# Mix-matrix strips made of three products each, two of them in column halves of the array

## The reference

```python
attn = einsum('ds,td->st', w1, w2) * sparse_mask        # 1024 x 1024, masked to a band
y    = einsum('bds,st->bdt', x, attn) + b2
x    = layernorm(x + gelu(y))
w_l  = dequant_kbit(qweight, lut4, 4)                   # 1024 x 1024 from 4 bit planes
w_h  = dequant_kbit(qweight, lut8, 8)
y    = where(norm(x) > 64, x @ w_h.T, x @ w_l.T) + bias
x    = layernorm(x + y)
```

## Time and profile before

| what | value |
|---|---|
| median of 3 executions | 307.67 us (307.31 to 307.9) |
| profiled execution, its own time | 306.75 us |
| its span | 304.9 us |
| PE busy | 289.1 us, 95% of the span |
| DVE busy | 196.3 us, 64% |
| ACT busy | 183.8 us, 60% |
| strip products (line 430) | 128 matmul records, from 5.00 to 35.11 us |
| mean granted TensorE clock | 0.994 of full speed |

### The profile page before, as it was taken

How to read it: one execution, slowest core, us unless ns; L and a number is a source line. 1 busy time by engine, 2 the same in 40 slices (tenths; PEclk the granted TensorE clock), 3 DMA queues, 4 the chain that set the end, 5 groups by cost and what they waited for, 6 DMA issues and landing times.

```text
span 304.9 us, 5064 instructions
## 1 busy us (share of the span) xinstructions
PE 289.1 (95%) x1907; PEld 254.0 (83%) x1907; DVE 196.3 (64%) x351; ACT 183.8 (60%) x244; POOL 108.8 (36%) x179
## 2 busy tenths in 40 slices
PE   7899889999999999999999999999999999999990
PEld 3688666676668999999999999999998888888880
DVE  2679998997858979798776785504035345344362
ACT  1965658888988968977895979342144453312210
POOL 4000003343343989898788100000033333323321
PEclk9999999999999999999999999999999999999997
DMA  6999998999999411011101111118237775443222
GB/s 222 398 355 354 379 383 265 244 255 231 206 186 202 93 35 37 34 37 34 37 34 38 52 38 52 53 37 231 115 121 250 264 257 200 170 157 153 103 111 107
DMA packets 28480, 49.78 MB, mean 163 GB/s; under 512 B 2464, under 2 KB 11936, under 8 KB 28448
## 3 DMA queue, kind: packets, MB, share of 16 engines
q1 hardware_dynamic: 23536, 40.79, 38.8%
q0 software_dynamic: 4352, 8.39, 15.3%
q10 hardware_dynamic: 560, 0.20, 0.2%
HBM read 36.79 MB, written 12.58 MB: 162 GB/s over the span
## 4 chain that ended last, share of the span: by engine, by line
PE 78%; DVE 10%; ACT 3%; issue 3%; DMA 3%; SPq 1%; POOL 1%; POOLq 0%; DVEq 0%; ACTq 0%
PE acc L559 19%; PE acc L561 19%; PE acc L560 19%; PE acc L542 5%; PE acc L430 3%; PE acc L488 3%; DMA w<-in_w2d 3%; PE acc L498 2%; PE acc L463 2%; PE acc L464 2%; PE acc L465 2%; DVE zz L1033 2%; DVE dest L991 1%; ACT z L706 1%; PE acc L475 1%
## 5 line engine op out<-in xcount | busy, mean ns | idle before, releaser
L559 PE MATMUL acc<-lin,zz 128*128 128x256 f32 (+2 forms) x424 | 130.4, 307 | 0.3 <-issue 0.3
L561 PE MATMUL acc<-lin,zz 128*128 128x256 f32 (+2 forms) x424 | 130.0, 307 | 0.0
L560 PE MATMUL acc<-lin,zz 128*128 128x256 f32 (+2 forms) x424 | 129.8, 306 | 0.0
L559 PEld LDWEIGHTS acc<-lin,zz 128*128 128x128 f32 x424 | 80.0, 189 | 4.6 <-issue 0.5
L560 PEld LDWEIGHTS acc<-lin,zz 128*128 128x128 f32 x424 | 80.3, 189 | 4.0
L561 PEld LDWEIGHTS acc<-lin,zz 128*128 128x128 f32 x424 | 80.2, 189 | 4.1
L724 ACT ACTIVATE leaf<-planes,lut,flip 128x1024 f32<-128x1024 uint8 x56 | 67.4, 1237 | 0.6 <-DVE dest L991 0.6
L991 DVE COPY_PREDICATED leaf<-planes,leaf 128x1024 f32<-128x1024 uint8 x32 | 43.4, 1355 | 12.0 <-ACT leaf L724 11.2
L1374 POOL DMA_DIRECT2D z<-in_xr x16 | 19.7, 1237 | 72.0 <-ACT z L706 70.1
L826 ACT ACTIVATE junk<-rows,cols 128x1024 bf16<-128x1024 f32 x15 | 17.2, 1150 | 41.3 <-POOL cols L1348 41.3
L1346 POOL TENSOR_TENSOR cols<-cols 128x1 f32<-128x1 f32 x15 | 9.5, 634 | 79.2 <-DVE rows L1109 79.2
(11 more groups left out here) (108 smaller groups left out, 431.9 us busy)
## 6 DMA issues: line engine op xcount, KB each, us to landing
z<-in_xt SPq DMA_DIRECT2D x16, 512.0 KB, 9.1
z<-in_xr POOLq DMA_DIRECT2D x16, 512.0 KB, 8.7
out_rows<-rows SPq DMA_DIRECT2D x15, 512.0 KB, 2.9
out_rows<-parts SPq DMA_DIRECT2D x32, 128.0 KB, 1.7
rows<-out_rows SPq DMA_DIRECT2D x16, 256.0 KB, 2.6
w<-in_w1d SPq DMA_DIRECT2D x7, 512.0 KB, 8.9
off_band<-in_mask_rest SPq DMA_DIRECT2D x8, 448.0 KB, 4.2
w<-in_w2d SPq DMA_DIRECT2D x3, 584.0 KB, 9.6
```

What stands on the lines that cost most here:

```text
L559: nc.tensor.matmul(bank, hi, w_hi, start=k == 0, stop=False)
L560: nc.tensor.matmul(bank, hi, w_lo, start=False, stop=False)
L561: last = nc.tensor.matmul(bank, lo, w_hi, start=False, stop=k == KB - 1)
```

## The change

Each strip's product with 272 columns is replaced by three: `strip_own`, all 128 rows of the strip with its own 128 columns; and in `strip_beside` up to two products whose weights are only 64 columns wide, rows 0 to 63 of the strip with the left 72 columns and rows 64 to 127 with the right 72. Their outputs lie on PSUM partitions 0 to 63 and 64 to 127, so they use the left and the right column half of the array. Strips 0 and 7 have one side product only. All own products of a row block of d stand together, and so do all side products; even row blocks begin with the own ones, odd row blocks with the side ones, so that the array changes between full width and half width once per row block and group of strips.

```diff
--- before.py
+++ after.py
@@ -425,29 +425,40 @@
                                             start=d == 0, stop=d == KB - 1)
                 last.then_inc(e_made, 1)
 
-            def strip_row(b, d):
-                first, end = strip_of(b)
-                return nc.tensor.matmul(unit_bank(b)[:, places_of(b)], w1[:, d, b * P:(b + 1) * P], w2[:, d, first:end],
-                                        start=d == 0, stop=d == KB - 1)
-
-            def front_strips():
-                starts = [first for first, _ in ROW_PIECES]
-                for d in range(KB):
-                    if d in starts:
-                        pe.wait_ge(w_loaded[starts.index(d)], 32)
-                    for b in range(FRONT):
-                        last = strip_row(b, d)
+            def strip_own(b, d):
+                return nc.tensor.matmul(unit_bank(b)[:, REACH:REACH + P], w1[:, d, b * P:(b + 1) * P],
+                                        w2[:, d, b * P:(b + 1) * P], start=d == 0, stop=d == KB - 1)
+
+            def strip_beside(b, d):
+                if b:
+                    nc.tensor.matmul(unit_bank(b)[0:SIDE, 0:REACH], w1[:, d, b * P:b * P + SIDE],
+                                     w2[:, d, b * P - REACH:b * P], start=False, stop=False)
+                if b + 1 < KB:
+                    nc.tensor.matmul(unit_bank(b)[SIDE:P, REACH + P:STRIP], w1[:, d, b * P + SIDE:(b + 1) * P],
+                                     w2[:, d, (b + 1) * P:(b + 1) * P + REACH], start=False, stop=False)
+
+            def strips(rows, bands):
+                for d in rows:
+                    if d % 2:
+                        for b in bands:
+                            strip_beside(b, d)
+                    for b in bands:
+                        last = strip_own(b, d)
                         if d == KB - 1:
                             last.then_inc(mix_made, 1)
+                    if d % 2 == 0:
+                        for b in bands:
+                            strip_beside(b, d)
+
+            def front_strips():
+                for n, piece in enumerate(ROW_PIECES):
+                    pe.wait_ge(w_loaded[n], 32)
+                    strips(range(*piece), range(FRONT))
 
             def back_strips(n):
-                for d in range(KB):
-                    if d % HALF_BLOCKS == 0:
-                        pe.wait_ge(w_loaded[len(ROW_PIECES) + 2 * n + d // HALF_BLOCKS], 32)
-                    for b in (FRONT + 2 * n, FRONT + 2 * n + 1):
-                        last = strip_row(b, d)
-                        if d == KB - 1:
-                            last.then_inc(mix_made, 1)
+                for h in range(2):
+                    pe.wait_ge(w_loaded[len(ROW_PIECES) + 2 * n + h], 32)
+                    strips(range(h * HALF_BLOCKS, (h + 1) * HALF_BLOCKS), (FRONT + 2 * n, FRONT + 2 * n + 1))
 
             def own(g, t):
                 if g:
```

## The result

The changed kernel takes 309.14 us (median of 5, 308.41 to 310.32) against 307.6 (5, 306.69 to 307.9): ratio 1.0055, 95% interval 1.003 to 1.0081. Its profiled execution took 308.41 us, with a span of 306.6 us. It is inside the stated range (307.0 to 311.5), but the forecast itself, no change, was wrong: the interval excludes it, and the median lies above the 307.2 to 308.2 that the prediction gave for this case.

A forecast was written before the change was run, and what follows sets the result against it. The prediction took DVE's list from `mask_strip(0)`, released by the mask load, as the bound. Path terms 0 + 0 + 0 on 306.75 us profiled, 307.67 by the median, gave 307.7 us, range 307.0 to 311.5.

The forecast's parts named there:

- What bounds the kernel: DVE's list from `mask_strip(0)` at 20.59 us up to `x_lo` sets the end; the mask load, landing at 20.55, releases it.
- Own products 0.111: PE's strips: each 128-column record of an own product takes 0.111 us, so 0.222 a product and 0.888 for four.
- side pairs abreast at 0.0625: PE's strips: two 72-column records on different column halves run together every 0.0625 us; a strip's two sides cost 0.125.
- A change of width at 0.2: PE's strips: each turn between full and half width costs 0.2 us, 24 turns in all; bounds 0 and 0.4.
- a dearer change: Rival in PE's strips: at 0.35 us per change of width, strip 6 completes at 38.03, kernel 309.3 us; chance 0.08.
- Nothing that DVE waits for moves: DVE still starts at 20.59 us with the mask load, strips 0, 4 and 6 are in time; path terms 0 + 0 + 0.
- the 448 instructions: Instructions added on PE, spread over 24 us in which nothing but the strips waits in its queue; no cost forecast.
- my rivals: Loads in turn 310.0 (0.26); dearer width change 309.3 (0.08); no overlap 320.7 (0.10), by page's rule (0.03); faster 307.1 (0.07).

The follow-up runs named there:

- the second: The changed kernel measured once more with no edit, against the kernel before: 308.59 us, ratio 1.0035 (1.0021 to 1.0049).
- the front half alone: Kernel before with only `front_strips` (strips 0 to 3) changed and `back_strips` as before: 308.92 us, ratio 1.0026 (1.0007 to 1.0044).
- 102 instructions: Kernel before, strips as they were, plus 102 early PE instructions (warm-up cut into 36 products, 12 one-column products ahead of each of two load waits): 308.8 us, 1.0044.
- the kernel without column halves: Changed kernel with side products on full-width weights (128 columns), otherwise the same: 316.9 us, ratio 1.0291 against the kernel before.
- the four runs with an early page in the table above: Kernel before with 102 more PE instructions (1.0044), changed kernel (1.0055), front changed only (1.0026), changed kernel again (1.0035); first instruction page at 14.4 to 16.1 us.

## Why the prediction was right and wrong

- **What bounds the kernel: right.** DVE's list behind `mask_strip(0)` sets the end, and that start hangs on the mask load. In the other profiles PE's last product moves by what the first token product moves, to within 0.25 us; the exception, by 0.45, is the kernel before with both mask halves earlier, whose load `xe_raw` (below) takes longest, 11.6 us.
- **Own products 0.111, side pairs abreast at 0.0625: right.** From the own products of one row block at 12.43 (`x16`, two row blocks in a row) to those at 15.55 are 3.12 us, 1.56 a row block against 1.588 forecast. The Trainium skill ("TensorE: Matmul & The Clock Gate", Part 3), that loads overlap with matmuls in flight only when the row group differs, does not hold here: two column halves on the same rows load and stream together.
- **A change of width at 0.2: slightly too dear.** Entering halves: own record to side record and to the next pair, 0.205 + 0.107 instead of 0.111 + 0.063, so 0.14; leaving 0.155 + 0.214 instead of 0.063 + 0.111, so 0.20. (By the prediction's own sums a dearer change would have decided from 0.28, by strip 6, and not from 0.29.)
- **"Nothing that DVE waits for moves": wrong, and this is the failed step.** I took the landing of the mask load (20.55) as fixed by SP's queue, and disposed of the 448 instructions by saying that nothing but the strips waits in PE's queue. That counts what an instruction costs on its engine and leaves out the DMA that brings it. The instruction page that used to come behind the mask's load now comes ahead of it, and the load lands 0.65 us later. None of my rivals had this; that the range held the time is luck, because it reached that far for rivals that did not happen.
- **The size.** 0.84 us at the first token product is 0.27% of the time. The first comparison had 0.55% (0.3 to 0.81), the second 0.35% (0.21 to 0.49), the front half alone 0.26%, 102 instructions 0.44%. Of what the medians show beyond 0.27% some parts are on record, and the rest is not settled. The slow last stores (0.8 us of the first two spans' difference) are chance.
- **A second late load.** Another 0.17 us of the first profile's difference at PE comes with a wait of DVE up to 75.4 us for `xe`, whose load `xe_raw` lands late. It looks like the same effect again, read off afterwards and not tested: issued at 62 to 63 us (in the kernel without column halves at 71.9), the load takes 10.9 to 11.6 us in the seven profiles in which an instruction page is fetched in its course or up to 0.9 us ahead of it, and 10.0 to 10.5 in the seven others. It falls differently in two executions of one program: the changed kernel fetches a page at 64.1 us in its first profile and at 58.3 in its second.
- **The clock.** In 8 of the 32 executions of the four runs with an early page in the table above, the granted clock over the span is 0.974 to 0.983, and they take 308.3 to 312.2 us; in none of the 201 other executions of the experiments, the kernel before among them, is it under 0.987. No profile is of such an execution, so where in the span the clock fell, and why in these runs, stays open.
- **The way of the delay** shows in part in the packets that the trace keeps with their times. Only the mask's loads have packets of 3200 bytes, 128 for half 0, eight for each of the 16 DMA engines if they share alike. In the two first profiles 120 of them are through at the same time, 19.45 before and 19.44 after. The last ends at 20.02 before and at 20.53 after, and after the change the last eight end one by one, 0.12 to 0.15 us apart, as the share of one late engine would. From the 120th to the last it is 0.74 to 1.19 us in the five profiles with an early page and the load in its old place, and 0.25 to 0.57 in the five with a late one; the landing follows 0.5 to 0.7 us behind the last packet. An instruction page is one packet of 1.14 us. At the 369 GB/s of this stretch one engine moves 16 KB in 16.4/(369/16) = 0.71 us, an estimate near the delay found. That the late engine is the one that carried the page is inferred: the packets have no engine's number.

## What to carry to other kernels

More instructions on an engine also mean earlier instruction pages, and those come through the DMA engines that bring the data: where a load under full DMA is the wait that decides, look at which side of it an instruction page falls. Before shortening work on an engine, find what its consumer waits for last; here nothing could be gained from the strips until the mask loads were moved, and then the next load or strip left 0.2 us to gain. Two profiles of one program differ by 0.6 us at the same instruction, so a difference of that size needs several of each. Where the packets of the load in question have a size of their own, their times tell more than the landing.

## What the runs showed of the hardware that I had not expected

- Column halves of the array work in parallel as row halves do: pairs of fp32 records with 72 columns every 0.0625 us, their loads starting within 0.01 us.
- One 16 KB page of instructions, fetched while the DMA queues are full, went with 0.84 us of a 308 us kernel, and with about 0.9 us more for a later load of 256 KB. The Trainium skill ("Runtime: NRT & Kernel Launch", Instruction fetch mechanics) calls the crossing of a 16 KiB boundary mostly hidden. The size agrees. Hidden it was for PE, whose idle times are ended by the same tiles and loads as before, but not for the load beside it.
- SP's last two DMA issues took 0.81 to 0.94 us in three profiles and 1.88 to 2.25 in the eleven others, of the same or nearly the same program.
